# Another PSUM bank and another place for the transposes that begin a blockwise inverse

## The chip, the cores and the metric

The kernel runs on one core of a Trainium2 chip. The core has five engines with a queue each: TensorE (PE, with its weight loads shown apart as PEld), VectorE (DVE), ScalarE (ACT), GpSimd (POOL) and SyncE (SP), which issues the DMAs. Each engine works through its own queue in order and waits on semaphores that the others raise. The metric is the device time of one execution in microseconds (us); lower is better. A measurement of this kernel tells about 0.3%, some 7 us, from no change.

## The reference

The model is one decoder block: a gated delta rule (linear attention) with 16 value heads over 8 batches of 256 tokens, then a cross attention, then a feed-forward part with block-scaled numbers. Only the first of the three matters here:

```python
q, k, v = split(silu(causal_conv(layernorm(x) @ W_qkv)))      # 8 key heads, 16 value heads of 128
beta = sigmoid(x @ W_b);  g = -exp(A_log) * softplus(x @ W_a + dt_bias)
def step(S, (qt, kt, vt, gt, bt)):
    S = S * exp(gt)
    v_adj = (vt - kt @ S) * bt
    S = S + outer(kt, v_adj)
    return S, qt @ S
o = rmsnorm(o) * norm_weight * silu(x @ W_z);  x = x + o @ W_out
```

The kernel does not walk over the tokens. It takes 128 tokens at once and needs for each block the inverse of a lower triangular 128 x 128 matrix.

## The kernel before, in words

`delta_rule` runs 33 steps: 8 key heads ("groups") times 4 pairs of batches, and one more step without projections that finishes the last pair. A step is software-pipelined: it computes the projections of the next pair (24 parts, `project`, lines 601 to 603: three matmuls of 512 columns each; four parts make one of six tiles) while it does the recurrence of the pair before. The last step of each group, and the first of the next, also carry the conversion of the next group's weights (`split`).

What a step does for the two batches s = 0 and 1, by engine:

- PE: `scores` (lines 623 to 630) gives k·k in `bank_a[s]` and q·k in `bank_b[s]`. Five projection parts follow, then `first_inverse`: sixteen transposes of 64 x 64 fp16 blocks of `inv_t` (line 650), written over the q·k scores in `bank_b[s]`. Then one part, `values` (line 640, eight full transposes of the values into `bank_a`), two parts, and six levels of the inverse. A level is `level_r` (line 666, sixteen small matmuls into `bank_c`) and `level_x` (lines 686 and 691, into `bank_b` and `bank_a`). Between `level_r` and `level_x` of the first level stands `to_channels` (line 759), four transposes for each batch that turn the outputs of the pair before into `proj[s]`; the second batch's needs tile 1 of the projections to have left `proj[1]`.
- DVE: per batch the masked k·k matrix, `a_t`, `a_half` and `inv_t` (line 1042, raises `x0_done[s]`); then `o_var`, the masked q·k (line 1048, `qk_done[s]`), and `silu` of the values (line 965, raises `silu_done`, for which `values` waits).
- ACT: the copies from PSUM in a fixed order: `kk_off`, then `qk_off` (line 864, raises `qk_off_done[s]`), tile 0 of the projections (lines 827 and 830), the transposed inverse `inv` (line 869, raises `t_done[s]`), the values `v_r` and `v` (lines 873, 874), `a_low` (877), tile 1 of the projections (827, 830), then the copies of the levels.
- POOL: normalises the outputs of the pair before (line 1181, raises `on_done[s]`, for which `to_channels` waits).

`first_inverse` may overwrite `bank_b[s]` only when ACT has copied `qk_off[s]`, so it waits for `qk_off_done[s]` beside `x0_done[s]`. `pe.sem_inc(quarter_go, 1)` stands ahead of each group of 64 x 64 tiles.

The order of every queue is written out by hand; nothing is reordered by a planner. The functions that the change touches:

Of the kernel before, what the change touches and what calls it, by code (L numbers as in the profile page):

```python
# [7 lines left out]
F16 = mybir.dt.float16  # L8
# [4 lines left out]
ACT = mybir.ActivationFunctionType  # L13
# [12 lines left out]
H = P // 2  # L26
HALVES = (slice(0, H), slice(H, P))
# [357 lines left out]
def delta_rule(nc, sh, W_qkv, W_z, out_t):  # L385
# [9 lines left out]
    with ExitStack() as st:  # L395
# [150 lines left out]
        with nc.Block() as block:  # L546
# [37 lines left out]
            def _(pe):  # L584
# [57 lines left out]

                def first_inverse(n):
                    for s in S:
                        pe.wait_ge(x0_done[s], n + 1)
                        pe.wait_ge(qk_off_done[s], n + 1)
                        pe.sem_inc(quarter_go, 1)
                        for hb in range(4):
                            for rows in HALVES:
                                last = pe.transpose(bank_b[s][rows, 0, :].bitcast(F16)[:, H * hb:H * hb + H],  # L650
                                                    inv_t[s][rows, hb, :], sh.ident16[rows, rows])
                        last.then_inc(t0_ps[s], 1)

# [16 lines left out]
                def level_x(n, l):  # L670
                    for s in S:
                        pe.wait_ge(r_done[s], LEVELS * n + l + 1)
                        if l == 0:
                            pe.wait_ge(v_done[s], n + 1)
                        else:
                            pe.wait_ge(x_done[s], LEVELS * n + l)
# [86 lines left out]
                def step(n, g, p):  # L763
                    projects = p is not None

                    def parts(first, last):
                        if projects:
                            project(n, g, p, first, last)

                    scores(n)  # L770
                    parts(0, 5)
                    first_inverse(n)
                    parts(5, 6)
                    values(n)
                    parts(6, 8)
                    for l in range(LEVELS):
# [43 lines left out]
            def _(act):  # L820
# [29 lines left out]
                def step(n, project, next_g):  # L850
# [11 lines left out]
                    for s in S:  # L862
                        act.wait_ge(qk_done[s], n + 1)
                        act.activation(qk_off[s][:, :], bank_b[s][:, 1, :], ACT.Copy).then_inc(qk_off_done[s], 1)
                    if project:
                        tile_copy(n, 0)
                    for s in S:
                        act.wait_ge(t0_ps[s], n + 1)
                        act.activation(inv[s][:, :, :].rearrange("p h c -> p (h c)"),
                                       bank_b[s][:, 0, :].bitcast(F16), ACT.Copy).then_inc(t_done[s], 1)  # L870
                    for s in S:
# [1567 lines left out]
```

## Time and profile before

| | us |
|---|---|
| median of 3 runs | 2410.67 |
| lowest, highest | 2406.59, 2412.37 |
| the profiled execution, its own time | 2405.05 |
| its span in the profile | 2403.3 |
| TensorE busy in the span | 2092.2 |
| VectorE busy | 1859.5 |
| ScalarE busy | 1433.9 |
| GpSimd busy | 1004.2 |
| mean granted TensorE clock | 0.954 of full speed |

The 33 steps of the delta rule lie between 77.5 and about 1570 us of the span. The profile lists for each instruction its start, its length, and, in brackets, how long its engine had been idle before it and what ended that. "PE idle ... issue" means that the profile shows no other engine's instruction as the releaser. Rows of neighbouring instructions of the same kind are merged, with their count behind x. "PEclk" is the granted clock of TensorE: 1.00 is 2.4 GHz and 0.50 is 1.2 GHz.

### The profile page before, as it was taken

The page shows a single profiled execution, that of the slowest core. Times are in us where ns is not written, and L with a number is a line of the kernel's source. Part 1 is how long each engine was busy: PE and PEld are TensorE (multiplying, and loading weights), DVE is VectorE, ACT ScalarE, POOL GpSimd, SP SyncE. Part 2 cuts the span into 40 slices and gives each one's busy share as a digit, 9 for nine tenths or more (in the row PEclk, how much of TensorE's full clock was granted, in tenths as well). Part 3 has the DMA queues.
Part 4 walks back from the last instruction along what each step waited for, and adds up shares of the span by engine and source line. Part 5 has one row for each costly group of instructions (what it writes and reads, how often), then busy time and mean ns, then how long its engine had stood idle before and what let it go on. Part 6 is the DMA issues. An engine that isn't in the chain of part 4 may idle for free. (4 is left out here: it accounts for less than half of the span.)

```text
span 2403.3 us, 56028 instructions
## 1 busy us (share of the span) xinstructions
PE 2092.2 (87%) x19224; PEld 1530.1 (64%) x19224; DVE 1859.5 (77%) x4187; ACT 1433.9 (60%) x3914; POOL 1004.2 (42%) x938
## 2 busy tenths in 40 slices
PE   5799999999999999998999999858988999756998
PEld 2576776776777777776777776645656666524444
DVE  8777877887777887777877877636888888764997
ACT  2466666666666666666666666536776777633333
POOL 7434334334234334234334234213566666650332
PEclk8799999999999999999999999769999999987999
DMA  2100000000000000000000000053333333113111
GB/s 73 49 9 22 30 9 22 31 9 22 31 9 22 31 9 22 31 9 22 31 9 22 31 9 22 19 164 90 97 97 90 94 85 96 52 44 121 56 55 51
DMA packets 122857, 107.56 MB, mean 45 GB/s; under 512 B 12080, under 2 KB 97072, under 8 KB 122800
## 3 DMA queue, kind: packets, MB, share of 16 engines
q1 hardware_dynamic: 122800, 106.87, 14.3%
q8 instruction: 28, 0.46, 0.1%
q14 instruction: 29, 0.24, 0.0%
HBM read 72.24 MB, written 34.60 MB: 44 GB/s over the span
## 5 line engine op out<-in xcount | busy, mean ns | idle before, releaser
L601 PE MATMUL proj<-xn_hi,w_lo 128*128 x768 | 362.6, 472 | 0.0
L958 DVE SCALAR_TENSOR_TENSOR qkv<-conv_in,taps,qkv 128x512 f32<-128x512 f32 x384 | 338.0, 893 | 8.9 <-ACT qkv L830 8.9
L602 PE MATMUL proj<-xn_lo,w_hi 128*128 x768 | 307.4, 400 | 0.2 <-issue 0.2
L603 PE MATMUL proj<-xn_hi,w_hi 128*128 x768 | 306.1, 399 | 0.0
L1202 POOL TENSOR_TENSOR r_norm<-sumsq,neg_half 128x8 f32<-128x8 f32 x32 | 67.3, 2102 | 517.3 <-DVE sumsq L1118 517.3
L1173 POOL TENSOR_TENSOR o_pow<-o_var,neg_half 128x4 f32<-128x4 f32 x68 | 89.4, 1332 | 412.6 <-DVE o_var L990 412.6
L1068 DVE TENSOR_TENSOR i_less_r<-bank_c,join_mask 128x256 f16<-128x256 f32 x330 | 124.4, 417 | 113.3 <-PE bank_c L666 112.9
L884 ACT ACTIVATE inv<-bank_b 128x256 f16<-128x256 f32 x330 | 111.5, 382 | 161.7 <-PE bank_b L686 161.4
L603 PEld LDWEIGHTS proj<-xn_hi,w_hi 128*128 128x128 f32 x768 | 146.1, 190 | 35.4
L601 PEld LDWEIGHTS proj<-xn_hi,w_lo 128*128 128x128 f32 x768 | 146.0, 190 | 25.9
L1188 POOL TENSOR_TENSOR g_mask<-mask_ge,gates 128x512 fp32r<-128x512 f32 x132 | 161.0, 1251 | 0.3 <-POOLq L506 0.3
L602 PEld LDWEIGHTS proj<-xn_lo,w_hi 128*128 128x128 f32 x768 | 147.4, 192 | 11.8 <-issue 0.7
L1663 ACT ACTIVATE probs<-ps_s,shift 128x256 f32<-128x256 f32 x256 | 118.0, 474 | 53.6 <-DVE shift L1784 52.6
L921 ACT ACTIVATE v_r<-v 128x256 fp32r<-128x256 f32 x66 | 27.6, 418 | 180.8 <-DVE v L1123 180.8
L2389 POOL TENSOR_TENSOR i_q<-i,i_scale 128x1024 bf16<-128x1024 fp8e4 x32 | 61.1, 1910 | 167.2 <-DVE i L2346 167.2
L1530 PE MATMUL ps_s<-k_blocks,q_t 128*128 128x512 f32 x256 | 129.0, 628 | 1.3 <-issue 1.1
L1495 PE MATMUL ps_y<-wo_hi,o_lo 128*128 128x512 f32 x256 | 108.8, 425 | 21.5 <-DVE wo_lo L1932 18.7
L1670 ACT ACTIVATE probs<-probs,r_sums 128x256 f32<-128x256 f32 x256 | 109.3, 500 | 26.4 <-DVE r_sums L1789 26.4
L686 PEld LDWEIGHTS bank_b<-i_less_r,inv_t 64*64 64x64 f16 x2640 | 71.0, 110 | 74.4 <-issue 74.1
L686 PE MATMUL bank_b<-i_less_r,inv_t 64*64 64x64 f16 x2640 | 97.8, 197 | 18.2 <-DVE i_less_r L1068 14.9
L2280 ACT ACTIVATE g_silu<-ps_g 128x512 f32<-128x512 f32 x64 | 38.2, 597 | 118.7 <-PE ps_u L2219 118.7
L2006 POOL TENSOR_TENSOR wq_y<-wq_raw,wq_inv 128x512 f32<-128x512 f32 x48 | 52.0, 1083 | 125.9 <-DVE wq_inv L1890 125.9
(288 smaller groups left out, 6103.1 us busy)
## 6 DMA issues: line engine op xcount, KB each, us to landing
out_t<-o_out SPq DMA_DIRECT2D x68, 256.0 KB, 2.0
o_raw<-out_t SPq DMA_DIRECT2D x32, 512.0 KB, 5.4
w_raw<-in_L_attn_W_qkv_dram SPq DMA_DIRECT2D x36, 256.0 KB, 2.8
wq_dram<-wq_q SPq DMA_DIRECT2D x48, 128.0 KB, 1.8
w_raw<-in_L_attn_W_z_dram SPq DMA_DIRECT2D x18, 256.0 KB, 2.7
x_sb<-in_x_dram SPq DMA_DIRECT2D x16, 256.0 KB, 2.7
x_in<-in_x_dram SPq DMA_DIRECT2D x16, 256.0 KB, 5.8
wq_raw<-in_L_ffn_w_gate_dram SPq DMA_DIRECT2D x16, 256.0 KB, 2.6
```

The costliest lines, as they stand in the source:

```text
L601: pe.matmul(out, w_lo[:, k, cols], sh.xn_hi[:, k, tok], start=(k == 0), stop=False)
L602: pe.matmul(out, w_hi[:, k, cols], sh.xn_lo[:, k, tok], start=False, stop=False)
L603: product = pe.matmul(out, w_hi[:, k, cols], sh.xn_hi[:, k, tok], start=False, stop=(k == KT - 1))
L686: last = pe.matmul(folded(bank_b[s])[rows, hb, :], inv_t[s][rows, hb, :], i_less_r[s][rows, hb, :], start=True, stop=True)
L884: act.activation(inv[s][:, :, :], folded(bank_b[s]), ACT.Copy).then_inc(t_done[s], 1)
L958: dve.scalar_tensor_tensor(out=out, in0=conv_in[:, j, :, k:k + T], scalar=taps[:, j, k:k + 1], in1=out, op0=ALU.mult, op1=ALU.add).then_in ...
L1068: dve.tensor_tensor(i_less_r[s][:, :, :], folded(bank_c[s]), bcast(sh.join_mask[:, l + 1, :], 1, 4), ALU.mult).then_inc(r_done[s], 1)
L1188: pool.tensor_tensor(g_mask[s][:, i, :, :], bcast(sh.mask_ge[:, :], 1, 4), bcast(g_cols, 2, P), ALU.mult).then_inc(mask_done[s], 1)
L1495: pe.matmul(ps_y[:, :], o_lo[e][:, g, :], wo_hi[:, k, :], start=begin, stop=False)
L1530: last = pe.matmul(ps_s[u][i][:, :], q_t[u][:, c, :], k_blocks[:, c, 2 * i:2 * i + 2, :], start=True, stop=True)
L1663: last = act.activation(probs[u][:, j, :], ps_s[u][j // 2][:, T * (j % 2):T * (j % 2) + T], ACT.Exp, bias=shift[u][:, j:j + 1], scale=SCAL ...
L1670: last = act.activation(probs[u][:, j, :], probs[u][:, j, :], ACT.Copy, scale=r_sums[u][:, j:j + 1])
```

## The change

PE: the transposes of `first_inverse` go to `bank_c[s]`, the bank that the first level's `level_r` uses, which has been free since DVE took the last step's outputs (`o1_done[s]`); so they wait for that instead of `qk_off_done[s]`. The wait for `qk_off_done[s]` moves to `level_x` of level 0, the next writer of `bank_b[s]`. The function takes one batch a call: batch 0 comes after two projection parts, batch 1 after five; the three parts after that all stand ahead of `values`.

ACT: the two copies `inv` (now from `bank_c`) come directly behind `kk_off`, ahead of tile 0 of the projections, and the two `qk_off` copies come behind tile 0.

```diff
-                def first_inverse(n):
-                    for s in S:
-                        pe.wait_ge(x0_done[s], n + 1)
-                        pe.wait_ge(qk_off_done[s], n + 1)
-                        pe.sem_inc(quarter_go, 1)
...
+                def first_inverse(n, s):
+                    pe.wait_ge(x0_done[s], n + 1)
+                    pe.wait_ge(o1_done[s], n + FIRST)
+                    pe.sem_inc(quarter_go, 1)
+                    for hb in range(4):
+                        for rows in HALVES:
+                            last = pe.transpose(bank_c[s][rows, 0, :].bitcast(F16)[:, H * hb:H * hb + H],
...
@@ level_x, l == 0
                             pe.wait_ge(v_done[s], n + 1)
+                            pe.wait_ge(qk_off_done[s], n + 1)
@@ step of PE
                     scores(n)
-                    parts(0, 5)
-                    first_inverse(n)
-                    parts(5, 6)
+                    parts(0, 2)
+                    first_inverse(n, 0)
+                    parts(2, 5)
+                    first_inverse(n, 1)
+                    parts(5, 8)
                     values(n)
-                    parts(6, 8)
@@ step of ACT, behind kk_off
                     for s in S:
+                        act.wait_ge(t0_ps[s], n + 1)
+                        act.activation(inv[s][:, :, :].rearrange("p h c -> p (h c)"),
+                                       bank_c[s][:, 0, :].bitcast(F16), ACT.Copy).then_inc(t_done[s], 1)
+                    if project:
+                        tile_copy(n, 0)
+                    for s in S:
                         act.wait_ge(qk_done[s], n + 1)
                         act.activation(qk_off[s][:, :], bank_b[s][:, 1, :], ACT.Copy).then_inc(qk_off_done[s], 1)
-                    if project:
-                        tile_copy(n, 0)
-                    for s in S:
-                        act.wait_ge(t0_ps[s], n + 1)
...
```

On PE, from the first inverse to the first level's `level_x`, before: `proj` rows are projection matmuls (three a part), line 650 is the first inverse, 640 the values, 666 `level_r`, 759 `to_channels`.

```order
L650 MATMUL bank_b<-ident,inv_t 64x64 x16
L601 MATMUL proj<-xn_hi,w_lo 128x512
L602 MATMUL proj<-xn_lo,w_hi 128x512
L603 MATMUL proj<-xn_hi,w_hi 128x512
L636 ISA
L640 MATMUL bank_a<-ident,qkv 128x128 x8
L601 MATMUL proj<-xn_hi,w_lo 128x512
L602 MATMUL proj<-xn_lo,w_hi 128x512
L603 MATMUL proj<-xn_hi,w_hi 128x512
L601 MATMUL proj<-xn_hi,w_lo 128x512
L602 MATMUL proj<-xn_lo,w_hi 128x512
L603 MATMUL proj<-xn_hi,w_hi 128x512
```

The same place on PE in the changed kernel, from the last of the three parts that now stand ahead of the values to the first projection part of the levels (line 649 is now the inverse, 665 is `level_r`):

```order
L603 MATMUL proj<-xn_hi,w_hi 128x512
L636 ISA
L640 MATMUL bank_a<-ident,qkv 128x128 x8
L655 ISA
L665 MATMUL bank_c<-inv,a_half 64x64 x16
L759 MATMUL proj<-ident,o 128x128 x4
L756 REGISTER_ALU
L759 MATMUL proj<-ident,o 128x128 x4
L686 MATMUL bank_b<-i_less_r,inv_t 64x64 x8
L691 MATMUL bank_a<-inv_t,i_less_r 64x64 x8
```

Two projection parts have moved from behind the values to ahead of them, and no projection matmul stands any more between the values and `level_x` of the first level.

On ACT, from the `kk_off` copies to the values, before:

```order
L861 ACTIVATE kk_off<-bank_a 128x128 x2
L864 ACTIVATE qk_off<-bank_b 128x128 x2
L822 ISA
L827 ACTIVATE conv_in<-proj 128x2x256
L830 ACTIVATE qkv<-proj,taps 128x512
L869 ACTIVATE inv<-bank_b 128x256 x2
L873 ACTIVATE v_r<-bank_a 128x256
```

And in the changed kernel:

```order
L862 ACTIVATE kk_off<-bank_a 128x128 x2
L865 ACTIVATE inv<-bank_c 128x256 x2
L823 ISA
L828 ACTIVATE conv_in<-proj 128x2x256
L831 ACTIVATE qkv<-proj,taps 128x512
L871 ACTIVATE qk_off<-bank_b 128x128 x2
L874 ACTIVATE v_r<-bank_a 128x256
```

`inv` and `qk_off` have changed places around tile 0; what follows, from the values on, stands in the same order.

## Rows read from the trace of the kernel before

**Rows 1.** Stretches, five steps: us, then busy time by engine, PEclk, DMA share, GB/s.

```profile
713.37:757.22 43.85, 40.98 (x457) 32.37 (x455) 34.85 (x85) 28.16 (x83) 17.32 (x17) 1.00 0.03 12
757.22:803.49 46.27, 41.18 (x457) 32.40 (x455) 38.30 (x91) 30.28 (x88) 17.61 (x17) 1.00 0.11 34
574.49:622.12 47.63, 42.57 (x456) 33.33 (x455) 38.33 (x91) 30.27 (x88) 17.61 (x17) 0.96 0.11 33
1165.37:1210.61 45.24, 41.04 (x455) 32.39 (x455) 36.03 (x88) 29.12 (x84) 17.31 (x17) 1.00 0.07 23
622.12:669.47 47.35, 43.55 (x454) 34.41 (x455) 34.81 (x88) 29.28 (x84) 16.43 (x17) 0.93 0.07 22
```

**Rows 2.** Timeline, first inverse of one step: start us, length us, engine, line, operation.

```profile
716.86 0.29 DVE L1042 TENSOR_TENSOR inv_t<-a_half,join_mask 128x256 f16<-128x256 f16 x1
...
717.22 0.40 PE L603 MATMUL proj<-xn_hi,w_hi 128*128 x1
...
719.32 0.40 PE L603 MATMUL proj<-xn_hi,w_hi 128*128 x1
719.64 0.29 DVE L1042 TENSOR_TENSOR inv_t<-a_half,join_mask 128x256 f16<-128x256 f16 x1
...
720.64 0.61 ACT L864 ACTIVATE qk_off<-bank_b 128x128 f32<-128x128 f32 x2 [2.58 <-DVE qk_diag L1048]
720.86 1.21 DVE L965 SCALAR_TENSOR_TENSOR qkv<-th,qkv 128x1024 f32<-128x1024 f32 x1
720.99 0.56 PEld L650 LDWEIGHTS bank_b<-ident,inv_t 64*64 64x64 f16 x16 [1.71 <-issue]
...
722.17 1.02 PEld L640 LDWEIGHTS bank_a<-ident,qkv 128*128 128x128 f32 x8
```

**Rows 3.** Timeline, a group of sixteen small tiles between two projection parts.

```profile
730.43 0.39 PE L603 MATMUL proj<-xn_hi,w_hi 128*128 x1
730.75 0.33 PEld L666 LDWEIGHTS bank_c<-inv,a_half 64*64 64x64 f16 x16 [0.36 <-issue]
...
731.12 0.19 PEld L601 LDWEIGHTS proj<-xn_hi,w_lo 128*128 128x128 f32 x1
...
731.69 0.40 PE L603 MATMUL proj<-xn_hi,w_hi 128*128 x1
```

**Rows 4.** Timeline, from the values to the first level, same step as rows 2.

```profile
723.03 0.39 ACT L873 ACTIVATE v_r<-bank_a 128x256 fp32r<-128x256 f32 x1 [0.17 <-PE bank_a L640]
...
723.28 2.04 POOL L1181 TENSOR_TENSOR o<-o,o_scale 128x512 f32<-128x512 f32 x2
...
724.76 0.33 PEld L666 LDWEIGHTS bank_c<-inv,a_half 64*64 64x64 f16 x16 [0.37 <-issue]
...
725.62 0.68 ACT L830 ACTIVATE qkv<-proj,taps 128x512 f32<-128x512 f32 x1
...
726.35 0.42 PEld L759 LDWEIGHTS proj<-ident,o 128*128 128x128 f32 x4 [0.81 <-ACT qkv L830]
...
726.94 0.20 PEld L686 LDWEIGHTS bank_b<-i_less_r,inv_t 64*64 64x64 f16 x8 [0.17 <-issue]
...
728.34 0.50 PE L601 MATMUL proj<-xn_hi,w_lo 128*128 x1
```

**Rows 5.** Stretches of 4 us, columns as rows 1: two ahead of falls, one quiet.

```profile
230.60:234.60 4.00, 2.41 (x54) 1.84 (x54) 4.00 (x6) 1.29 (x5) 1.87 (x2) 1.00 0.04 9
626.50:630.50 4.00, 1.98 (x9) 1.26 (x7) 3.78 (x16) 1.28 (x3) 0.09 (x1) 1.00 0.02 6
724.40:728.40 4.00, 3.24 (x75) 2.27 (x73) 2.48 (x5) 3.01 (x9) 4.00 (x4) 1.00 0.17 65
```

**Rows 6.** The stretch of 3.4 us behind the first of those falls, columns as rows 1.

```profile
234.60:238.00 3.40, 3.40 (x38) 1.94 (x38) 2.48 (x5) 1.69 (x4) 0.00 (x0) 0.50 0.23 69
```

**Rows 7.** Timeline of PE, the waits that lie in the first two stretches of rows 5.

```profile
233.49 0.31 PE L686 MATMUL bank_b<-i_less_r,inv_t 64*64 64x64 f16 x8 [1.59 <-DVE i_less_r L1068]
...
631.14 0.39 PE L650 MATMUL bank_b<-ident,inv_t 64*64 64x64 f16 x7 [2.67 <-issue]
```

More of the change, by code:

```diff
@@ L641, in values @@
                         last.then_inc(v_ps[s], 1)
-                def first_inverse(n):
-                    for s in S:
-                        pe.wait_ge(x0_done[s], n + 1)
-                        pe.wait_ge(qk_off_done[s], n + 1)
-                        pe.sem_inc(quarter_go, 1)
[L648 to L652, printed above, removed]
+                def first_inverse(n, s):
[5 more added lines that the diff above has]
+                            last = pe.transpose(bank_c[s][rows, 0, :].bitcast(F16)[:, H * hb:H * hb + H],
+                                                inv_t[s][rows, hb, :], sh.ident16[rows, rows])
+                    last.then_inc(t0_ps[s], 1)
                 def level_r(n, l):
@@ L862, in step @@
                     for s in S:
-                        act.wait_ge(qk_done[s], n + 1)
-                        act.activation(qk_off[s][:, :], bank_b[s][:, 1, :], ACT.Copy).then_inc(qk_off_done[s], 1)
+                        act.wait_ge(t0_ps[s], n + 1)
+                        act.activation(inv[s][:, :, :].rearrange("p h c -> p (h c)"),
+                                       bank_c[s][:, 0, :].bitcast(F16), ACT.Copy).then_inc(t_done[s], 1)
                     if project:
@@ L867, in step @@
                     for s in S:
-                        act.wait_ge(t0_ps[s], n + 1)
-                        act.activation(inv[s][:, :, :].rearrange("p h c -> p (h c)"),
-                                       bank_b[s][:, 0, :].bitcast(F16), ACT.Copy).then_inc(t_done[s], 1)
+                        act.wait_ge(qk_done[s], n + 1)
+                        act.activation(qk_off[s][:, :], bank_b[s][:, 1, :], ACT.Copy).then_inc(qk_off_done[s], 1)
                     for s in S:
```

## The prediction, made blind

> **What bounds the kernel now.** I read the stretches by step first. A plain step lasts 43.85 us and TensorE is busy for 40.98 of them; no other engine passes 34.85 [rows 1]. The steps repeat to within a few hundredths, so one step can stand for all. Steps at a group's end carry the weight conversion (46.27 us), those at a group's start carry its rest (45.24) [rows 1]. TensorE sets the pace, but with holes, and what matters is which engine closes each hole.
>
> The timeline of one step shows two holes near the change. First, PE is through five projection parts (last matmul at 719.32) and loads the inverse's first transposes only at 720.99, when the first `qk_off` copy (begun 720.64) is there; `inv_t` of batch 0 was ready at 717.15 and of batch 1 at 719.93 [rows 2]. Second, `to_channels` of batch 1 is loaded at 726.35, after ACT has finished tile 1's copy at 725.62 + 0.68 = 726.30; `level_x` follows at 726.94 [rows 4].
>
> **The first hole, and what takes its place.** From 719.32 to the values' load at 722.17 are 2.85 us [rows 2]. The same sequence without a wait costs 0.32 us for the change to small tiles (730.43 to 730.75), 0.37 for sixteen tiles (to 731.12) and 0.57 for the part behind them (to 731.69) [rows 3], 1.26 together. So 1.59 us of wait stand there, and the change removes them: batch 0's transposes find `inv_t` long ready. For batch 1, PE would be at 717.22 + 0.44 (first group of eight) + 3 x 0.70 (parts; 719.32 less 717.22 is three of them [rows 2]) + 0.32 = 720.08, and `inv_t` is ready at 719.93: no wait, with 0.15 to spare for the semaphore.
>
> Against that PE now does two more parts ahead of the values, 2 x 0.70 = 1.40 us, and enters the small-tile form twice instead of once. A group of sixteen costs 1.26 less the part's 0.70 = 0.56 us, of which the tiles themselves are 0.25 to 0.33 (the loads last 0.33 [rows 3]); the second entry is thus 0.23 to 0.31, and I take 0.3 because it includes draining and refilling. Sum at the values: -1.59 + 1.40 + 0.30 = **+0.11 us**; they load at 722.28 instead of 722.17. They could not gain much in any case: they wait for `silu`, which DVE ends at 720.86 + 1.21 = 722.07 [rows 2], and DVE's queue is not touched. The bounds are -0.05 and +0.2 us a step.
>
> **Why the two parts' time is not won back behind the values.** `level_r` can now start about 1.2 us earlier (723.6 instead of 724.76 [rows 4]), and so can DVE's first masking. But `level_x` is behind `to_channels` in PE's queue, and batch 1 of that waits for ACT. ACT's chain from `v_r` at 723.03 to 726.30 is 3.27 us of copies back to back: two `v_r`, two `v`, two `a_low` and tile 1 [rows 4]. Its head is `values`, 0.86 us after their load. ACT's reordering wins nothing there: it takes `inv` earlier and ends tile 0 and `qk_off` about 0.5 us before it is needed, but then waits for the values. So `level_x` comes at 726.94 + 0.11 = 727.05, and all that follows moves with it. The 1.59 us wait is moved to `to_channels`: PE finishes batch 0's four transposes near 724.9 (they wait for POOL's first half, 723.28 + 1.02 = 724.30 [rows 4]) and idles until 726.46. Over 31 steps (the 32 with projections but the first, which runs at the low clock): 31 x 0.11 = **+3.4 us**. `qk_off`'s later end (about 722.5) is ahead of `level_x` by over 4 us; the wait added there costs nothing. `o1_done` is an event of the last step's end. No DMA moves; the store of batch 0 may go out a little earlier, on SP, which nobody waits for.
>
> **The clock.** Without a fall of the clock a group end lasts 46.27 us at 1.00, with one 47.63 at 0.96: 1.36 us a fall; a group start 45.24 against 47.35 at 0.93: 2.11 [rows 1]. It fell in 6 of 8 group ends and in 2 of 7 group starts, to 0.50, the level of 1.2 GHz [rows 6], and in none of the plain steps. What PE did before: in the 4 us ahead of the first of these falls it was busy for 2.41, with a 1.59 us wait between small tiles; ahead of one at a group start 1.98, with a 2.67 us wait [rows 5, 7]. The other five falls at group ends show 2.39 to 2.42. The thinnest stretch of a plain step, 724.40 to 728.40, is busy for 3.24 and never lost the clock [rows 5].
>
> The changed order makes a thinner one in every step. The last projection matmul ends near 722.4 and the next comes at 728.34 + 0.11 [rows 4]; between stand the values, sixteen small tiles, four transposes, 1.6 us of nothing, four transposes, small tiles. In the 4 us from 723.4, PE is busy for 0.44 + 0.66 + 0.66 + 0.34 = 2.1 us (an estimate from the lengths in this step, a little generous since tiles overlap), between the 1.98 and 2.41 of the places that fell. Of 15 such places 8 fell, so a thin place does not always pull the clock down. For 31 new ones I take 13, less than half, because a fall shifts the steps behind it. 13 x 1.36 = **+17.7 us**. At group starts the 2.67 us wait is cut in two (batch 0 waits about 1.1 us, batch 1 about 0.5), so the two falls there go: 2 x 2.11 = **-4.2 us**.
>
> Sum: 3.4 + 17.7 - 4.2 = +16.9 us on the profiled time of 2405.05, 2422. That execution lies 5.6 below the median of 2410.67, within the spread of the three runs; on the median the forecast is 2428.
>
> **A rule that weighs against these rows.** The Trainium skill, page "TensorE: Matmul & The Clock Gate", section "Why this matters for your kernels", ties a throughput drop in mid-kernel to an idle gap between matmul bursts longer than any in the changed order; by it the new falls do not come and the sum is the first rival's. The trace disagrees: the clock fell behind a wait of 1.59 us [rows 7]. The same page, section "Part 4: PE-mode transpose", says that transposes do not count as busy in the way matmuls do; by it the new stretch is nearly empty and the second rival holds. The trace is against it, as far as it goes: the quiet stretch of rows 5 held eight full transposes and small tiles alone for most of its length and kept the clock.
>
> **Rivals.** (a) The thin stretch does not pull the clock down more often than before. For it: transposes and tiles are work, and the stretch is cut by them; the estimate of 2.1 has no exact precedent with transposes. Then 3.4 us, less 4.2 at the group starts: 2410.67 - 0.8 = 2410, or 2404 to 2417 with the falls at group ends shifting by a few. (b) It falls in nearly every step, 28 times: 3.4 + 28 x 1.36 - 4.2 = +37, 2448; more if some falls last twice as long, as at 622.12. (c) The other side, faster: the wait does vanish. It needs tile 1's copy to end before PE gets to batch 1, at about 725 instead of 726.30, so that `level_x` follows `level_r` at once. Price 1.26 us x 31 = -39, 2372. It decides if ACT's copies of the values could start a microsecond earlier; against it stands `silu` at 722.07, which no edit moves. (d) The change doesn't do what it says, the transposes still waiting for something late: `inv_t` of batch 1 leaves 0.15 us, so at most a tenth or two a step, +3 to +6, inside (a) or the forecast.
>
> **How the numbers follow.** Forecast (8 to 18 added falls, 2418 to 2440): 0.45. (a) 0.31. (b) 0.16. (c) 0.05, a rest of 0.03 for shifts of falls in later stages. Slower by over 0.3%: 0.45 + 0.16 + 0.01 = 0.62; within 0.3% (about what a measurement of this kernel can tell from no change): 0.32; faster: 0.06. The range of 8 in 10 takes in (a) from about 2407 and (b) up to 2450.
>
> **What would show it.** In the changed profile: the inverse's wait on PE gone, and in its place about 1.6 us ahead of line 759's second group, released by ACT's tile 1 copy; a plain step with a full clock of 43.9 to 44.05 us; steps with PEclk below 1.00 also among the plain ones, each about 1.4 us longer. It is wrong if plain steps get shorter, if `level_x` comes earlier against the start of its step, or if no plain step shows a fallen clock.

## The result, and the profile after

| | before | changed |
|---|---|---|
| median of 20 runs, us | 2407.8 | 2415.3 |
| lowest | 2403.87 | 2408.18 |
| ratio, changed to before | | 1.0037, 95% interval 1.0023 to 1.0051 |
| profiled execution, its own time | 2405.05 | 2424.6 |
| mean granted TensorE clock in it | 0.954 | 0.936 |

One of the changed kernel's runs, 3378.0 us at a clock of 0.55, was disturbed: the median of 2415.3 still counts it, while the other 19, whose mean the ratio compares, have a median of 2414.4 and a mean of 2416.7. The changed kernel is thus slower by 7 to 9 us, 0.37% by the ratio. The interval (0.23 to 0.51%) excludes no change, but it does not lie wholly above the 0.3% that a measurement of this kernel can tell. The 19 runs fall into two groups: eleven of 2408.2 to 2416.2 us and eight of 2422.5 to 2425.0 us, 12.7 us apart in the mean. The profiled execution belongs to the upper one, so it shows more than the change costs at the median. A second measurement of the same kernel (`e8_changed_again`, below) has a profile from the lower group, at 2415.35 us. I read the two profiles together.

The head of the page, changed kernel:

```profile
span 2422.9 us, 56094 instructions
PE 2123.5 (88%) x19224; PEld 1549.4 (64%) x19224; DVE 1855.6 (77%) x4187; ACT 1432.0 (59%) x3914; POOL 999.4 (41%) x938
```

PE is busy for 31 us more than before, though it executes the same matmuls; DVE, ACT and POOL are within 5 us of before. That fits matmuls that ran at a lower clock. The next view says in which steps. Six steps of the changed kernel (us, busy time of PE, PEld, DVE, ACT and POOL, PEclk, DMA share, GB/s): a plain step at full clock, one with one stretch at the low clock, one with two; a group end at full clock and one with a fall; a group start with two. A stretch at the low clock lasts 3.4 us, two of them 6.8.

```profile
309.76:353.57 43.81, 41.08 (x456) 32.33 (x455) 34.59 (x85) 28.04 (x83) 17.24 (x17) 1.00 0.03 12
353.57:398.42 44.85, 42.31 (x457) 33.27 (x455) 34.92 (x85) 28.12 (x83) 16.80 (x17) 0.96 0.03 12
719.13:765.31 46.18, 43.65 (x456) 34.07 (x455) 34.85 (x85) 28.21 (x83) 16.79 (x17) 0.93 0.03 11
398.42:444.62 46.20, 41.27 (x456) 32.34 (x455) 38.02 (x91) 30.17 (x88) 17.55 (x17) 1.00 0.11 34
215.73:261.99 46.26, 42.57 (x456) 33.30 (x455) 37.95 (x91) 30.33 (x88) 17.54 (x17) 0.96 0.11 34
261.99:309.76 47.77, 43.86 (x454) 33.98 (x455) 35.68 (x87) 29.01 (x84) 17.24 (x17) 0.93 0.07 22
```

Against [rows 1]: the plain step at full clock has not become longer (43.81 against 43.85, the mean of before's sixteen is 43.87), and plain steps now lose the clock, which none did before. The rows of the group ends hold a surprise. There a fall of one stretch costs 0.06 us here, where it cost 1.36 before.

From windows like these I made the table on which most of what follows rests: the 31 steps behind the first, sorted by kind. "Fallen" counts steps with a mean clock below 1.00.

| | before | changed | changed, 2nd profile |
|---|---|---|---|
| 31 steps, us | 1401.0 | 1418.8 | 1409.9 |
| 16 plain, us (fallen) | 702.0 (0) | 718.5 (13) | 716.7 (13) |
| 8 group ends (fallen) | 378.2 (6) | 369.6 (5) | 375.1 (8) |
| 7 group starts (fallen) | 320.8 (2) | 330.8 (7) | 318.0 (2) |
| plain step at full clock | 43.87 | 43.81 | 43.79 |

Of the 19.6 us between the profiled executions 17.8 lie in these steps, and of the 10.3 us in the second profile 8.9. The two profiles of one kernel differ mostly in the group starts (seven fallen against two, 12.7 us); the group ends go the other way by 5.5 us. All 25 and all 23 falls begin between 12.9 and 16.2 us into their step, at the changed place. None is left where the eight of before began: 21.4 to 22.0 us into a group end, 8.3 or 8.4 us into a group start.

Now the changed place itself. Timeline of the changed kernel, in the plain step that begins at 309.76, with the columns of [rows 2]:

```profile
316.49 0.20 PEld L649 LDWEIGHTS bank_c<-ident,inv_t 64*64 64x64 f16 x8 [0.37 <-issue]
...
316.84 0.39 ACT L865 ACTIVATE inv<-bank_c 128x256 f16<-128x256 f16 x1 [2.11 <-PE bank_c L649]
...
317.26 1.21 DVE L966 SCALAR_TENSOR_TENSOR qkv<-th,qkv 128x1024 f32<-128x1024 f32 x1
...
318.70 1.03 PEld L640 LDWEIGHTS bank_a<-ident,qkv 128*128 128x128 f32 x8
...
319.56 0.38 ACT L874 ACTIVATE v_r<-bank_a 128x256 fp32r<-128x256 f32 x1 [0.94 <-PE bank_a L640]
...
320.71 0.42 PEld L759 LDWEIGHTS proj<-ident,o 128*128 128x128 f32 x4 [0.49 <-POOL o L1182]
...
322.15 0.68 ACT L831 ACTIVATE qkv<-proj,taps 128x512 f32<-128x512 f32 x1
...
322.89 0.42 PEld L759 LDWEIGHTS proj<-ident,o 128*128 128x128 f32 x4 [1.76 <-ACT qkv L831]
...
323.47 0.20 PEld L686 LDWEIGHTS bank_b<-i_less_r,inv_t 64*64 64x64 f16 x8 [0.17 <-issue]
```

The second batch's first inverse (316.49) stood idle for 0.37 us, what the change to small tiles costs in [rows 3] too. The wait of [rows 2] is gone. The values are loaded 318.70 - 309.76 = 8.94 us into the step, against 722.17 - 713.37 = 8.80 before. The new hole is ahead of the second `to_channels`: its loads idle for 1.76 us until ACT has tile 1 out. The 4 us that hold this hole, in a step that then lost the clock and in the one shown above, which kept it, and the 3.4 us behind the first:

```profile
362.90:366.90 4.00, 2.10 (x31) 1.59 (x29) 1.55 (x4) 3.27 (x8) 4.00 (x7) 1.00 0.00 0
319.50:323.50 4.00, 2.10 (x31) 1.42 (x29) 1.51 (x3) 3.27 (x8) 4.00 (x6) 1.00 0.06 22
366.90:370.30 3.40, 3.39 (x54) 2.76 (x54) 1.99 (x4) 1.32 (x4) 3.40 (x4) 0.50 0.41 154
```

PE is busy for 2.10 us in both, between the two places that fell before [rows 5]. The same stretch, then, is sometimes followed by a clock of 0.50 and sometimes not.

### The profile page after: what moved, and what is told of

Its sections match the earlier page's. It is cut to its first block and busy times, and to the rows that moved or that the text cites. A ratio compares the mean times of both kernels' runs of the same rounds, so it can differ in the third digit from the quotient of the medians.

```text
span 2422.9 us, 56094 instructions
## 1 busy us (share of the span) xinstructions
PE 2123.5 (88%) x19224; PEld 1549.4 (64%) x19224; DVE 1855.6 (77%) x4187; ACT 1432.0 (59%) x3914; POOL 999.4 (41%) x938
## 5 line engine op out<-in xcount | busy, mean ns | idle before, releaser
L601 PE MATMUL proj<-xn_hi,w_lo 128*128 x768 | 370.8, 483 | 0.0
L959 DVE SCALAR_TENSOR_TENSOR qkv<-conv_in,taps,qkv 128x512 f32<-128x512 f32 x384 | 331.3, 876 | 0.0
L602 PEld LDWEIGHTS proj<-xn_lo,w_hi 128*128 128x128 f32 x768 | 150.8, 196 | 10.9
L686 PE MATMUL bank_b<-i_less_r,inv_t 64*64 64x64 f16 x2640 | 103.3, 205 | 6.2 <-DVE i_less_r L1069 5.8
L759 PE MATMUL proj<-ident,o 128*128 128x128 f32 x272 | 50.1, 314 | 66.7 <-ACT qkv L831 48.9
```

Source lines behind the costliest of these rows:

```text
L601: pe.matmul(out, w_lo[:, k, cols], sh.xn_hi[:, k, tok], start=(k == 0), stop=False)
L602: pe.matmul(out, w_hi[:, k, cols], sh.xn_lo[:, k, tok], start=False, stop=False)
L686: last = pe.matmul(folded(bank_b[s])[rows, hb, :], inv_t[s][rows, hb, :], i_less_r[s][rows, hb, :], start=True, stop=True)
L959: dve.scalar_tensor_tensor(out=out, in0=conv_in[:, j, :, k:k + T], scalar=taps[:, j, k:k + 1], in1=out, op0=ALU.mult, op1=ALU.add).then_in ...
```

## The experiments

Two theories stood against each other at first. One: the changed order costs nothing by itself, and all of its loss is the clock, which the hole at `to_channels` pulls down. The other: the two parts moved ahead of the values make every step later, and the clock adds to it. Each ratio below is to the kernel before on the same chip, with its 95% interval.

**The two parts put back behind the values** (e1_parts_back).

```diff
-                    parts(5, 8)
+                    parts(5, 6)
                     values(n)
+                    parts(6, 8)
```

> The changed kernel with the two projection parts put back behind the values (0-2, batch 0, 2-5, batch 1, 5-6, values, 6-8); bank, split and ScalarE's order as changed. Theory (the changed kernel's cost is the clock, which falls in the stretch that has lost its projection matmuls): no plain step shows a fallen clock, plain steps last 43.7 to 43.9 us, the falls at group starts (a 2.67 us wait before) are gone too, falls at group ends stay at 4 to 6; 2400 to 2406 us against 2407.8 before. Rival (the second entry into small tiles and the moved copies cost by themselves, 0.1 to 0.3 us a step): plain steps 44.0 to 44.2 at full clock and 2411 to 2417 us.

Measured: 2400.18 us, ratio 0.9973 (0.9962 to 0.9983). The wait ahead of the second `to_channels` is back to 0.80 us (0.81 before), and no plain step falls (0, 6 and 0 fallen of plain steps, ends and starts). So those two parts cost the changed kernel 15 us. The rest of the change gains 6 us over before, and the sums say where. The plain steps give 1.1 us (43.81 each), the group starts 4.7, the group ends nothing.

**Work in the hole, order unchanged** (e2_filler). Twelve matmuls of 128 columns, whose products nobody reads, stand ahead of the second batch's `to_channels`.

```diff
+                def filler(n):
+                    pe.wait_ge(qk_off_done[0], n + 1)
+                    for i in range(12):
+                        pe.matmul(bank_b[0][:, 3, :], w_hi[:, i % 4, 0:P], sh.xn_hi[:, i % 4, 0:P], start=True, stop=True)
...
                     for s in S:
+                        if s == 1 and projects:
+                            filler(n)
```

> The changed kernel with twelve matmuls of 128 columns, whose result nobody reads, put on TensorE between the two batches of the output transposes, where it idles 1.6 us for ScalarE's copy of tile 1. Adds work, takes none away. Theory (thin work there makes the clock fall): the plain steps keep the full clock and last 43.8 to 44.0 us, falls from about 30 to under 10, 2398 to 2408 us. Rival 1 (the falls have another cause): as many falls as the changed kernel, 2408 to 2425 us. Rival 2 (the extra matmuls last longer than the hole): 0.1 to 0.5 us a step more, 2415 to 2430 us.

Measured: 2396.61 us, ratio 0.9952 (0.9938 to 0.9966), with 0, 3 and 0 steps fallen. The place in that kernel's trace, first its 4 us and then its timeline:

```profile
312.95:316.95 4.00, 3.38 (x43) 2.80 (x41) 1.50 (x3) 3.28 (x8) 4.00 (x6) 1.00 0.06 22
```

```profile
314.16 0.66 PE L766 MATMUL proj<-ident,o 128*128 128x128 f32 x4 [0.38 <-POOL o L1189]
314.57 1.53 PE L755 MATMUL bank_b<-xn_hi,w_hi 128*128 128x128 f32 x12
316.34 0.65 PE L766 MATMUL proj<-ident,o 128*128 128x128 f32 x4 [0.23 <-ACT qkv L838]
```

This is the cleanest of the runs on the clock. PE gets more work and the plain step at full clock stays where it was (43.84 against 43.81), yet the kernel is 19 us faster. All that was added is activity in the thin stretch, 3.38 us of 4 instead of 2.10. The falls, and not the order, are what the changed kernel loses by. Whether the idle time counts, or the lack of full-size matmuls, this run alone does not tell, since it changes both.

**Only the bank and ACT's order** (e4_bank_only): both batches again behind five parts, and two parts behind the values, as before.

```diff
-                    parts(0, 2)
+                    parts(0, 5)
                     first_inverse(n, 0)
-                    parts(2, 5)
                     first_inverse(n, 1)
-                    parts(5, 8)
+                    parts(5, 6)
                     values(n)
+                    parts(6, 8)
```

> Bank and ScalarE's order as changed, but the transposes of both batches stand together after five projection parts and the parts behind them as before. Theory: TensorE gets to batch 0 at 6.3 us of the step and to batch 1 at 6.7, the values are then held by VectorE's silu at 8.70, so plain steps last 43.75 to 43.85 us as in e1_parts_back, and the split by batch is worth under 2 us in all: 2400 to 2407 us. Rival (the split is what counts): over 5 us slower than e1_parts_back.

Measured: 2398.19 us, ratio 0.9964 (0.9949 to 0.9978). Its plain step of 43.81 us is that of e1: splitting the two batches is worth nothing there. 0, 3 and 3 steps fell.

**`to_channels` behind the first `level_x`** (e5_channels_late), on top of e1. If the copy of tile 1 held the step up, `level_x` would now come earlier.

```diff
                         level_r(n, l)
-                        if l == 0:
-                            to_channels(n, projects)
                         parts(at, at + after_r)
                         level_x(n, l)
+                        if l == 0:
+                            to_channels(n, projects)
```

> e1_parts_back with the output transposes behind the first level's second half instead of ahead of it, so that this half no longer stands behind ScalarE's copy of tile 1. Theory (ScalarE's in-order chain of copies up to tile 1 at 12.94 us of the step holds the first level): the first level's products are ready early but ScalarE copies them only behind tile 1; level 1 begins at 13.8 instead of 14.5 us, VectorE's output gate then takes part of it back: plain steps 43.2 to 43.7 us, 2388 to 2402 us. Rival (VectorE's gated outputs hold level 1 fully): plain steps unchanged at 43.8, 2400 to 2408 us.

Measured: 2402.46 us, ratio 0.9983 (0.9974 to 0.9992), plain step 43.81; the rival held. `level_x` of the first level came 1.25 us earlier than in e1 (12.11 against 13.36 us into the step) and it was worth nothing. The lead was lost at once, on DVE. Its gated outputs stand between the maskings of the first and the second level and wait for `to_channels`, which now comes last (step from 303.01):

```profile
316.61 1.41 DVE L999 SCALAR_TENSOR_TENSOR o_out<-proj,norm_half,z_silu 128x512 f32<-128x512 f32 x2 [1.30 <-PE proj L759]
317.94 0.75 DVE L1070 TENSOR_TENSOR i_less_r<-bank_c,join_mask 128x256 f16<-128x256 f32 x2
```

The second level's masking begins 14.93 us into the step, 0.34 later than in e1, and yet the step is as long. In this kernel PE runs 3.3 us (314.20 to 317.51) of small tiles and transposes alone, with no wait longer than 0.48 us, and no plain step fell. So such work by itself did not pull the clock down over that length; in the changed kernel the stretch without a full-size matmul is 6.0 us long (318.93 to 324.92), and no run had a stretch that long without the wait.

With e1 and e2 this asked a question of its own. The step's plain length hardly moves, whether the values' first transpose comes 0.27 us earlier (e1) or 0.14 us later than before, and whether the second level's masking begins at 14.60 us (e1, e4), 14.81 (before) or 14.94 (changed, e2). Something further on resets it.

I followed single instructions through plain steps at full clock. `level_r`'s third result is masked by DVE (third level) 18.32 us into the step before and 18.30 in e3 (below), and 18.25 to 18.27 in the changed kernel, e1, e2, e4 and e5. Up to there the kernels differ. What stands ahead of that masking, in before (step from 713.37), DVE and POOL:

```profile
728.84 2.92 DVE L958 SCALAR_TENSOR_TENSOR qkv<-conv_in,taps,qkv 128x512 f32<-128x512 f32 x2
731.69 0.74 DVE L1068 TENSOR_TENSOR i_less_r<-bank_c,join_mask 128x256 f16<-128x256 f32 x2
```

```profile
727.72 4.94 POOL L1188 TENSOR_TENSOR g_mask<-mask_ge,gates 128x512 fp32r<-128x512 f32 x4
```

The same in e1 (step from 304.93):

```profile
320.20 3.07 DVE L960 SCALAR_TENSOR_TENSOR qkv<-conv_in,taps,qkv 128x512 f32<-128x512 f32 x2
323.19 0.74 DVE L1070 TENSOR_TENSOR i_less_r<-bank_c,join_mask 128x256 f16<-128x256 f32 x2
```

```profile
319.23 4.93 POOL L1190 TENSOR_TENSOR g_mask<-mask_ge,gates 128x512 fp32r<-128x512 f32 x4
```

Two steps of the convolution, 0.75 us each elsewhere, take 3 us together while POOL multiplies the gates. POOL begins 14.35 us into the step before and 14.30 in e1, by its own queue. The pair on DVE began 15.47 and 15.27 into the step and ended at 18.39 and 18.34: what it had gained it lost again. So DVE was held by POOL. Seen singly, the first of the two convolution steps and POOL's first two products, in e1 (step from 304.93) and in the changed kernel (step from 309.76):

```profile
320.20 1.62 DVE L960 SCALAR_TENSOR_TENSOR qkv<-conv_in,taps,qkv 128x512 f32<-128x512 f32 x1
319.23 2.04 POOL L1190 TENSOR_TENSOR g_mask<-mask_ge,gates 128x512 fp32r<-128x512 f32 x2
325.38 1.27 DVE L959 SCALAR_TENSOR_TENSOR qkv<-conv_in,taps,qkv 128x512 f32<-128x512 f32 x1
324.06 2.04 POOL L1189 TENSOR_TENSOR g_mask<-mask_ge,gates 128x512 fp32r<-128x512 f32 x2
```

The convolution step begins 15.27 us into the one and 15.62 into the other and ends at 16.89 in both, 0.55 us behind the end of POOL's second product (16.34). That is how a difference of 0.35 us is wiped out. What is left of one, 18.32 against 18.25, goes with POOL's own start: 14.35 in before and e3, which have ACT's old order, 14.29 to 14.32 in the others.

The theory that came out: this hold, and neither the inverse's wait nor `to_channels`, sets when a plain step of these kernels goes on. It can be tested by moving POOL's products and nothing else.

**POOL's gate products moved behind `z_silu`** (e6_gates_late, on top of e1), some 8 us later.

```diff
                             pool.wait_ge(d_ps[s], n + 1)
+                        pool.wait_ge(z_done, n + 1 + FIRST)
                         mask_gates(n + 1)
```

> e1_parts_back with GpSimd's four products g_mask (14.3 to 19.3 us of a step) held until VectorE's z_silu of the step, about 22.7 us. In every order so far, before, changed and e1 to e5, the third masking of VectorE begins at 18.25 to 18.32 us, whatever the first level did, and the two taps ahead of it take 1.46 us each instead of 0.75 while GpSimd's products run. Theory (GpSimd's products hold VectorE's taps and so reset each step's lead at 18.3 us): the taps take 0.75 each, level 2 begins 0.8 to 1.4 us earlier, a plain step lasts 42.6 to 43.5 us, 2365 to 2393 us. Rival 1 (the taps are long for a reason of their own): no change, 2397 to 2403. Rival 2 (the slow-down only moves to what VectorE does from 22.7 to 27.7 us): 2395 to 2410.

Measured: 2371.33 us, ratio 0.9854 (0.984 to 0.9869), 29 us less than e1 by the edit of one line. Not one of the 31 steps fell, and the plain step is 43.42 us. Some 8 of the 29 us are the six falls at e1's group ends, which are gone with PE's wait there (1.7 us in e1, ended 20.2 us into the step; none in e6); the rest is shorter steps, 0.39 us a plain one and 1.1 a group end. The place in its trace (step from 300.85):

```profile
316.10 1.41 DVE L960 SCALAR_TENSOR_TENSOR qkv<-conv_in,taps,qkv 128x512 f32<-128x512 f32 x2
318.38 0.76 DVE L1070 TENSOR_TENSOR i_less_r<-bank_c,join_mask 128x256 f16<-128x256 f32 x2 [0.87 <-PE bank_c L665]
```

```profile
323.25 5.25 POOL L1190 TENSOR_TENSOR g_mask<-mask_ge,gates 128x512 fp32r<-128x512 f32 x4 [8.07 <-DVE z_silu L1008]
```

The pair takes 1.41 us, and the masking behind it now waits for PE (0.87 us of idle time) and not PE for it. It comes 17.53 us into the step instead of 18.26. The conflict isn't gone, it lies elsewhere. The `silu` pair that now runs beside the products takes 2.69 us, against 1.29 in e1; nobody waits for it at once:

```profile
324.92 2.69 DVE L967 SCALAR_TENSOR_TENSOR qkv<-th,qkv 128x512 f32<-128x512 f32 x2 [0.22 <-ACT th L904]
```

**The same with `to_channels` late as well** (e7_channels_gates_late): the edits of e5 and e6 together.

> e5_channels_late with the same later products of GpSimd. Theory: with the reset at 18.3 us gone, the earlier first level counts for the first time: 0.1 to 0.5 us a step less than e6_gates_late. Rival (VectorE's gated outputs ahead of level 1 take the lead back): the same as e6_gates_late within 3 us.

Measured: 2370.26 us, ratio 0.9846 (0.9832 to 0.9861), plain step 43.34, 0.08 below e6, just under the 0.1 to 0.5 expected. Of all the kernels here it has the lowest time, 1.5% below the one before, though its interval and that of e6 overlap, so that the two cannot be told apart.

**The changed kernel a second time** (e8_changed_again), with no edit.

> The changed kernel once more, for a second profile. Its 19 runs lie in two groups, 2408 to 2416 and 2422 to 2425 us, with a mean granted clock of 0.941 to 0.945 and 0.936 to 0.938. Theory (the groups differ in how many steps lose the clock, and nothing else): full-clock plain steps last 43.81 us again, one fall of one period costs 1.0 us in a plain step, and an execution near 2410 has 6 to 10 low periods fewer than the profiled one of 2424.6. Rival (another order-related cost varies): plain steps at full clock differ between executions.

Measured: 2413.49 us, ratio 1.0031 (1.0017 to 1.0045). The full-clock plain step is 43.79 us, as expected. 23 steps fell where the first profile had 25, with 31 stretches at the low clock against 33, where I had expected 6 to 10 fewer. So the two executions don't differ by the number of falls as much as I had thought, but by where they land: 2 of 7 group starts against 7, and 8 of 8 group ends against 5. One of these seven runs, 2418.2 us, lies between the two groups.

**ACT's old order with the new bank and the new order on PE** (e3_act_old_order): `qk_off`, tile 0, `inv`.

```diff
-                        act.wait_ge(t0_ps[s], n + 1)
-                        act.activation(inv[s][:, :, :].rearrange("p h c -> p (h c)"),
-                                       bank_c[s][:, 0, :].bitcast(F16), ACT.Copy).then_inc(t_done[s], 1)
+                        act.wait_ge(qk_done[s], n + 1)
+                        act.activation(qk_off[s][:, :], bank_b[s][:, 1, :], ACT.Copy).then_inc(qk_off_done[s], 1)
```

> The changed kernel with ScalarE's old order (qk_off, tile 0, inv). Theory: the inverse's copies are ready at 8.8 us of the step, the first level starts at 10.2 in both orders, so ScalarE's part of the change is worth nothing: 2408 to 2425 us like the changed kernel, with the same falls. Rival (taking inv early counts): over 5 us slower than the changed kernel.

Measured: 2424.45 us, ratio 1.0076 (1.0061 to 1.009), 11 us above the changed kernel in the same comparison. My theory had no loss here, and the rival (over 5 us slower) is nearer. At full clock the order is worth almost nothing, 43.86 against 43.79 us a plain step, some 2 us over 31. The rest lies in what the falls cost: 11, 6 and 6 steps fell, where e8 has 13, 8 and 2. The changed kernel's first profile, with 7 fallen group starts, took 2424.6 us, so one such profile of e3 does not show that the order sends the falls there; all four of its runs (2421.7 to 2427.6 us) are near or in the upper group of the changed kernel, and why I could not settle.

**Gates late in the kernel before** (e9_before_gates_late), and with the three other orders: the changed one (e10_changed_gates_late), with the filler (e11_filler_gates_late) and e4's (e12_bank_gates_late). Each is that kernel with the one line of e6. If the hold of POOL hid the lead and lag of the orders, the orders must differ once it is gone.

> The kernel before with nothing changed but GpSimd's four products held until z_silu. Theory (the reset at 18.3 us was all that hid a lead or a lag of the first level): level 1's masking begins at 14.8 here against 14.6 in e1_parts_back, and this 0.2 us now counts: plain steps 43.6 us against 43.42 in e6_gates_late, and group starts may lose the clock in their 2.67 us wait: 2374 to 2382 us. Rival (the order around the inverse is worth nothing with the reset gone either): 2368 to 2373 us.

> The changed kernel, GpSimd's products held until z_silu. Theory: its level 1 begins at 14.95, 0.35 us behind e1_parts_back, and its thin stretch stays: plain steps 43.75 us at full clock, with falls in about two of three steps, at 1.0 to 1.4 us each now that no hold takes a part back: 2390 to 2415 us. Rival (the falls were tied to the old step length and thin out): under 2385 us.

> e2_filler (changed kernel, twelve unread matmuls in the hole) with GpSimd's products held until z_silu: both causes taken away from the changed order, so what remains is its lag of 0.35 us at level 1. Theory: plain steps 43.7 to 43.8 us, no falls there, 2376 to 2386 us. Rival: as fast as e6_gates_late within 3 us, which would say that the changed order has no lag of its own.

> e4_bank_only (other bank, ScalarE's new order, both batches' transposes together) with GpSimd's products held until z_silu. Theory (the split by batch is worth nothing, since the values wait for silu either way): plain steps 43.40 to 43.45 us and 2368 to 2374 us, as e6_gates_late. Rival: the split counts once nothing resets the lead, 0.1 us a step or more against e6_gates_late.

| order on PE | with the hold: median, plain step | gates late: median, plain step | gates late: fallen |
|---|---|---|---|
| before | 2407.8, 43.87 | 2386.95, 43.62 | 0, 0, 3 |
| changed | 2415.3, 43.81 | 2416.13, 43.76 | 11, 6, 7 |
| changed, filler | 2396.61, 43.84 | 2383.38, 43.76 | 0, 0, 0 |
| bank only (e4) | 2398.19, 43.81 | 2377.32, 43.41 | 0, 0, 4 |
| parts back (e1) | 2400.18, 43.81 | 2371.33, 43.42 | 0, 0, 0 |

The ratios of e9 to e12 are 0.9917 (0.99 to 0.9935), 1.0043 (1.0029 to 1.0057), 0.9901 (0.9881 to 0.9921) and 0.9883 (0.9861 to 0.9904). The four plain steps came as expected. The medians of e9, e10 and e12 lie 5, 1 and 3 us above their ranges: the falls at their group starts cost e12 5.2 us and e9 3.8, and I had counted none in e12. A plain step at full clock of e9, of e10 and of e12:

```profile
305.88:349.51 43.63, 40.92 (x457) 32.36 (x455) 34.69 (x85) 28.11 (x83) 17.67 (x17) 1.00 0.03 12
```

```profile
489.60:533.36 43.76, 41.04 (x456) 32.34 (x455) 34.59 (x85) 27.98 (x83) 17.61 (x17) 1.00 0.03 12
```

```profile
301.99:345.39 43.40, 41.04 (x456) 32.26 (x455) 34.61 (x85) 28.08 (x83) 17.61 (x17) 1.00 0.03 12
```

With the hold, five orders lie within 0.07 us a step. Without it they spread over 0.35, and in the order that the second level's masking gives. Against before, the changed order lags by 0.14 us a step, near the +0.11 of the prediction. The new bank and ACT's new order, which take away the old wait for `qk_off`, are worth 0.21 together (e9 against e12). Even so the changed order gains nothing from late gates in all. At full clock its 31 steps are 6.7 us shorter (e11, without a fall, has 1379.9 us, against 1386.6 worked out below with the hold). But 24 steps still fall, and they now cost 1410.7 - 1379.9 = 30.8 us, 7.5 more than in e8. The filler alone, with the plain step unchanged at 43.76, is worth 33 us there.

## Why the prediction was right in kind and wrong in size

**What held.** The place of the waits came out as worked out. Batch 1's first inverse waits for nothing but the change to small tiles. The values come 0.14 us later in the step (worked out: 0.11). The hole went to `to_channels`, released by ACT's tile 1. The stretch around it is busy for 2.10 us of 4 (worked out: 2.1). Plain steps lose the clock, 13 of 16. The prediction gave "slower by over 0.3%" a chance of 0.62, and the ratio is 0.37%, though its interval reaches below 0.3%. That the low clock does it, and not the order, is shown by e2: work that nobody needs, in the hole, takes 19 us off.

**The number.** The forecast of 2428 us stands 12.7 above the measured median of 2415.3. 2.9 of that is its base, a median of three runs, 2410.67 against 2407.8 for twenty. The measured 2415.3 lies outside the forecast's own 2418 to 2440 and inside the 2404 to 2417 of rival (a), whose mechanism is out, so the time alone would have pointed to the wrong cause. One of the prediction's own signs of being wrong also came: plain steps at full clock got shorter, 43.81 us, and not 43.9 to 44.05.

**The rule set beside the rows.** In 25 steps of the changed kernel the clock fell, and the longest wait of PE at the place is the one shown, 1.76 to 1.78 us for the loads. The Trainium skill, page "TensorE: Matmul & The Clock Gate", section "Why this matters for your kernels", ties such a drop to a longer gap; by it none of these falls would have come, and the trace disagrees.

**What failed, first step: "all that follows moves with it", 31 x 0.11 = +3.4 us.** At full clock the changed kernel's 31 steps would sum to 16 x 43.81 + 8 x 46.20 + 7 x 45.15 = 1386.6 us. Before's would sum to 1401.0 less its own falls (6 x 1.36 + 2 x 2.11 = 12.4), 1388.6. The changed order is thus 2.0 us faster at full clock, not 3.4 slower: 5.4 of the 8 us by which the forecast of +16.9 stands above the second profile's +8.9. The lag is real where it was worked out, and it ends some 8 us later in the step, where DVE stands beside POOL's gate products in every order. I followed the lag up to `level_x` and took it from there to the end of the step. The trace had the answer: DVE's pair of 2.92 us at 728.84, twice its usual length. e10 against e9 shows 0.14 us a step as soon as POOL is out of the way.

**Second step: 13 falls at 1.36 us.** The forecast had 13 new falls and kept the six at the group ends of before. At the new place 25 steps fell in the profiled execution and 23 in the second profile, about twice the 13, and the six of before are gone. "Less than half" was read from places that were busier (2.39 to 2.42 us of 4, for the most part) than the new one (2.10). In the second profile the falls cost 1409.9 - 1386.6 = 23.3 us, 1.01 for each fallen step; net of before's 12.4 that is +10.9, where the forecast has 17.7 - 4.2 = 13.5. In the profiled execution they cost 1418.8 - 1386.6 = 32.2 us, 1.29 for each, net +19.8. So the clock's term looks nearly right because too few falls and too high a price cancel in part, which is luck. The price depends on the place and on the length. One stretch of 3.4 us at the low clock costs 1.0 us in a plain step (44.80 against 43.81), 1.0 at a group start, 0.06 at a group end (46.26 against 46.20). Two stretches, as in 8 of the fallen steps of either profile, cost 2.4 us in a plain step (46.20), 2.4 to 2.7 at a group start (47.52 to 47.81) and 0.9 at a group end (47.15 against 46.20). The 1.36 was read from group ends of before, where the clock fell 21 us into the step, behind the hold. The new falls at group ends begin at 12.9 to 14.6 us, ahead of it, and PE's lateness goes into a wait that is there anyway: 20.2 us into the step PE waits 1.36 to 1.38 us for DVE in the three group ends of the profiled execution that did not fall, and 0.09 to 0.31 in the five that did. That this hides it is shown by e10 too, where gates are late. Group ends with a fall and without one, in that kernel:

```profile
396.75:443.36 46.61, 42.57 (x457) 33.32 (x455) 37.88 (x91) 30.29 (x88) 18.37 (x17) 0.96 0.11 34
...
578.24:623.77 45.53, 41.28 (x456) 32.34 (x455) 37.81 (x91) 30.20 (x88) 18.37 (x17) 1.00 0.11 35
```

1.08 us for a fall, 0.06 with the hold in place.

**Third: "at group starts ... the two falls there go", -4.2 us.** In e1 they do, and the starts are 4.7 us shorter. In the changed kernel the old falls are gone too, but the starts have the new hole, and 2 of 7 fall in one profile, 7 of 7 in the other. That difference is 12.7 us, as much as the two groups of runs are apart; with one profile of each I can't show that it is what parts them, and the group ends differ by 5.5 the other way. It also explains why the forecast looked good beside the profiled execution (+19.6) and was too high beside the median. A single execution of a kernel whose clock falls often is a poor yardstick.

**The rivals.** (a), no more falls, is out. (b), 28 new falls at 1.36 us, was nearer in their number, with 25 and 23 at the new place, and too dear: they cost 1.0 to 1.3, and six of the old ones, which it kept, are gone. (c), the faster one, priced an earlier `level_x` at 1.26 us a step and wanted ACT's copies earlier for it. e5 brought `level_x` forward by 1.25 us without them, which gained nothing; with POOL's products out of the way (e7) it gained 0.08 us a step over e6. DVE's gated outputs, which wait for `to_channels`, take the rest. The 0.39 us a step that e6 gains over e1 is POOL's.

## What to carry to other kernels

A lag or a lead is worth counting only up to the next wait that something else sets: before multiplying it by the number of steps, follow the same instruction in the trace to the end of the step, and look for operations on the way that take twice their usual time. When waits are moved on TensorE, add up how busy the few microseconds around the new place are; where transposes and small tiles are all that is left, the hole can cost more through the clock than the old wait did. The price of a fall is to be read at a place with the same slack behind it.

## What the runs showed of the hardware that I had not expected

DVE and POOL slow each other down. The durations of before's convolution step on DVE and of the gate product on POOL, and of the latter in e1 (least, median and greatest of all, in ns):

```profile
L958 DVE SCALAR_TENSOR_TENSOR qkv<-conv_in,taps,qkv x384: 735/747/1525, 89.0 to 1525.4; 128x512 f32<-128x512 f32 x192
```

```profile
L1188 POOL TENSOR_TENSOR g_mask<-mask_ge,gates x132: 1030/1050/1504, 71.0 to 1496.8; 128x512 fp32r<-128x512 f32 x132
```

```profile
L1190 POOL TENSOR_TENSOR g_mask<-mask_ge,gates x132: 1030/1482/1491, 71.1 to 1490.0; 128x512 fp32r<-128x512 f32 x132
```

Alone 0.75 us, beside the other about 1.5; POOL's product goes from 1.03 to 1.48 us. Of its four in a plain step the first two keep 1.03 to 1.06 in both kernels and the last two take 1.48 to 1.50, so the median (1050 or 1482) only says which side of the half it fell on. DVE's maskings, which read one operand from PSUM, take 0.41 us in the same stretch as elsewhere (the least of all in before is 0.41, the greatest 0.43). The Trainium skill, page "SBUF — State Buffer", section "Who interferes with whom", says that a DVE instruction with two SBUF inputs contends with a GpSimd instruction that reads SBUF, and that one holds the shared port for its whole length while the other is blocked. The rows agree on which instructions suffer, and in kind with the blocking: the second product keeps its 1.04 us, while the convolution step beside it takes 1.27 to 1.62, by when it began, and ends 0.55 us behind that product in e1 and in the changed kernel alike. Then the two engines take turns. Full exclusion over the whole recorded lengths they don't show: one step and one product behind each other would be 0.75 + 1.03 = 1.78 us, and here a pair goes through in 1.45 (the third and fourth products of e1 begin 1.45 us apart). Some part of each must overlap the other.

Moving POOL's four products by 8 us, behind a point where DVE's slowed work has nobody waiting, gave 20 to 32 us in four orders, 13 in the one with the filler and none in the changed one. A clock that falls behind some stretches and not behind others that look the same (2.10 us busy in both) remains unexplained.
